# A graph kernel's first two sage passes: TensorE takes the next layer's rows directly behind the turn of the gathered rows

## The reference

```python
def _sage_conv(h, src, dst, Ws, Wn, b):
    msg = h[src]
    summed = jax.ops.segment_sum(msg, dst, num_segments=n)
    deg = jax.ops.segment_sum(jnp.ones(src.shape), dst, num_segments=n)
    neigh = summed / jnp.maximum(deg, 1.0)[:, None]
    return h @ Ws.T + neigh @ Wn.T + b
h = jax.nn.relu(_sage_conv(x, src, dst, Ws0, Wn0, b0))
prev = h
h = _sage_conv(h, src, dst, Ws1, Wn1, b1)
h = jax.nn.relu(h + prev)
return _sage_conv(h, src, dst, Ws2, Wn2, b2)
```

## Time and profile before

| what | value |
|---|---|
| median of 3 runs | 5097.33 us (5092.68 to 5098.29) |
| the profiled execution, its own time | 5105.29 us |
| its span in the profile | 5103.5 us |
| PE busy | 3761.0 us (74%) |
| DVE busy | 3758.0 us (74%) |
| ACT busy | 3214.3 us (63%) |
| POOL busy | 2811.2 us (55%) |
| granted TensorE clock, mean | 0.862 |

### The profile page before, as it was taken

One profiled execution on the slowest core, in us unless ns is written; L12 is line 12 of the kernel. 1 busy time (PEld: TensorE's weight loads), 2 busy tenths in 40 slices (PEclk: granted clock), 3 DMA queues, 4 the chain that ended last, 5 costly groups with the idle time before them and its releaser, 6 DMA issues. The chain is left out here.

```text
span 5103.5 us, 104447 instructions
## 1 busy us (share of the span) xinstructions
PE 3761.0 (74%) x23663; PEld 3105.7 (61%) x23663; DVE 3758.0 (74%) x10843; ACT 3214.3 (63%) x11475; POOL 2811.2 (55%) x2759
## 2 busy tenths in 40 slices
PE   6365889966877677768776878788687887967775
PEld 5254778855557555645674655466576776856664
DVE  1576789978869786978796868699576775746666
ACT  2022779966868686968674533278586785646554
POOL 0474767702750473067104767676564765757776
PEclk9699999988998898989776767699899998978777
DMA  8899999955975696579664446567697996762221
GB/s 177 111 290 282 363 370 312 279 146 158 287 255 148 194 285 212 161 229 291 187 183 137 152 149 206 168 215 240 211 304 254 302 305 214 246 153 59 65 66 55
DMA packets 918273, 1074.23 MB, mean 210 GB/s; under 512 B 202779, under 2 KB 565065, under 8 KB 917106
## 3 DMA queue, kind: packets, MB, share of 16 engines
q1 hardware_dynamic: 763570, 890.24, 53.5%
q0 software_dynamic: 90944, 180.06, 14.4%
q10 hardware_dynamic: 63556, 1.81, 1.8%
HBM read 509.54 MB, written 566.14 MB: 211 GB/s over the span
## 5 line engine op out<-in xcount | busy, mean ns | idle before, releaser
L2366 POOL DMA_INDIRECT H<-gat_rows,src_i x784 | 802.4, 1023 | 870.0 <-POOLq L80 631.9
L1917 POOL DMA_INDIRECT s_G<-sage_rows,src_i x588 | 603.1, 1026 | 353.7 <-issue 162.5
L1696 POOL DMA_INDIRECT r_G<-rel_rows,idx x392 | 404.8, 1033 | 166.5 <-issue 117.4
L2555 PE MATMUL p_M<-Wg,p_hT 128*128 128x132 f32 x2352 | 340.3, 289 | 61.1 <-DVE p_res L2612 47.2
L2555 PEld LDWEIGHTS p_M<-Wg,p_hT 128*128 128x128 f32 x2352 | 294.8, 194 | 108.1 <-issue 91.7
L2612 DVE SCALAR_TENSOR_TENSOR p_res<-p_M,p_rr,cg 128x132 f32<-128x132 f32 x1176 | 333.8, 346 | 2.8 <-PE p_M L2555 1.9
L1709 PE MATMUL r_t<-r_oh,relv 8*128 8x512 f32 x294 | 205.3, 784 | 171.2 <-DMA r_G<-rel_rows,idx 72.8
L1305 PE MATMUL d_S<-ones,d_sqT 128*128 128x1 f32 x1568 | 226.1, 265 | 138.6 <-DVE d_ve L1450 138.5
L2694 PEld LDWEIGHTS p_pl_p<-Wn,p_pl_h 128*128 128x128 f32 x1568 | 202.3, 195 | 206.5 <-ACT p_pl_h L2788 159.6
L2694 PE MATMUL p_pl_p<-Wn,p_pl_h 128*128 128x128 f32 x1568 | 221.2, 286 | 137.4 <-ACT p_pl_h L2788 137.3
L1305 PEld LDWEIGHTS d_S<-ones,d_sqT 128*128 128x128 f32 x1568 | 219.5, 216 | 165.9 <-issue 128.3
(11 more groups left out here) (483 smaller groups left out, 12421.8 us busy)
## 6 DMA issues: line engine op xcount, KB each, us to landing
gat_rows<-p_res SPq DMA_DIRECT2D x294, 264.0 KB
sage_rows<-p_pl_s SPq DMA_DIRECT2D x294, 256.0 KB
gat_rows<-x_row SPq DMA_DIRECT2D x98, 536.0 KB
gat_rows<-d_res SPq DMA_DIRECT2D x147, 264.0 KB
d_hs<-gat_rows SPq DMA_DIRECT2D x147, 256.0 KB
s_hT<-sage_slots_t SPq DMA_DIRECT2D x147, 256.0 KB
slot_rows<-H SPq DMA_DIRECT2D x49, 544.0 KB
x_x<-in_x SPq DMA_DIRECT2D x98, 256.0 KB
```

The lines of the kernel that those rows point to most:

```text
L1696: pool.indirect_dma_start(self.G[:, g % 4, k, :], None, table, bass.IndirectOffsetOnAxis(index[:, c:c + 1], 0), bounds_check=bound, oob_is ...
L1917: pool.indirect_dma_start(self.G[:, g % 4, k, :], None, kn.st[self.l], bass.IndirectOffsetOnAxis(kn.idx[:, c:c + 1], 0), bounds_check=boun ...
L2366: pool.indirect_dma_start(kn.H[:, c, 0:width], None, table, bass.IndirectOffsetOnAxis(index[:, c:c + 1], 0), bounds_check=bound, oob_is_er ...
L2555: mm = pe.matmul(self.pM[self.bank(b, j)][:, k // 2, (k % 2) * TW:(k % 2 + 1) * TW], self.hT[l][:, b.s2, k * P:(k + 1) * P], kn.Wg[:, l, : ...
```

## The change

One number in `SageSlots.tensor`: the place of `rows` in the turn of PE, for the two passes that are not the last.

```diff
         if self.last:
             return [(sum_squares, 5), (own, 2), (turn_back, 5), (turn, 1), (rows, 5)]
-        return [(turn, 1, kn.KG, 1), (rows, 4, kn.KG, 4), (own, 2, kn.KG, 3)]
+        return [(turn, 1, kn.KG, 1), (rows, 4, kn.KG, 1), (own, 2, kn.KG, 3)]
```

## The result

The changed kernel takes 5028.19 us (median of 4 runs, 5021.91 to 5035.27), the kernel before 5097.81 us (median of 4, 5092.68 to 5102.47). The ratio is 0.9862, with a 95% interval of 0.9849 to 0.9876: faster by 1.4%, 70 us. The forecast was 60 us less, 5037 us.

The account below looks back on a forecast made before the run. A circle of waits through PE and DVE was taken to set 6.04 us per turn; 82 x (6.04 - 5.35) = 56.6 us plus 3.6 for tails gives 60, so 5097.33 - 60 = 5037 us, range 5024 to 5070.

Parts of the forecast that it names:

- The circle and the gap: PE and DVE in s0 and s1: `rows` leaves the waiting circle, 0.89 us, and fills PE's idle 0.70 us.
- `rows` doesn't wait in its new place: PE's `rows` behind the turned rows: ACT's results come 1.8 us ahead, so the cost is 0.
- Rival B: No change, 5097 us: `rows` would wait for ACT and hold up PE's transposes, 0.8 us a turn; chance 0.06.
- PE and DVE alone: Turn in s0 and s1 allowed by these two engines: 5.17 + 0.06 = 5.23 us.
- the back edge of the loop: Every fourth turn: DVE starts `own` 0.49 us behind PE, not 0.20, costing 0.06 us on the mean.
- that fits by 0.06 us: PE's own step: `add_own` ends at S + 2.21, with 0.14 us for the semaphore, before own at S + 2.41.
- POOL: Issuing four gathers a turn in s0 and s1 takes 5.26 us, so PE can't get far below this.
- The DMA engines: Transfers of 1.84 MB per turn in s0 and s1: taken as 5.35 us, between 5.26 and 5.46.
- Tails and heads: Turns outside the 41 of each pass: three tail turns each give 6 x 0.6 = 3.6 us, heads nothing.
- What it would show: Signs in s0 and s1: turns of 5.3 to 5.4 us, `base` wait small, PE waiting for gathers, 340 to 350 GB/s.
- Rival C: Slower, up to 5163 us: ACT waits for the store of `features` from its two buffers; chance 0.05.

Follow-up runs that it names:

- Experiment 1: The changed kernel with `rows` last in PE's turn, behind `products`, instead of behind the turned rows; 5027.91 us, ratio 0.9883 to the kernel before.
- experiment 3: The changed kernel with `rows` moved in pass s0 only, s1 keeping the old order; 5044.44 us, ratio 0.9917 to the kernel before.
- Experiment 4: The kernel before, with two of the four matmuls of the turned gathered rows made twice in s0 and s1; 5081.24 us, ratio 0.9995.
- experiment 6: The changed kernel with two of the four matmuls of the turned gathered rows made twice in s0 and s1; 5007.13 us, ratio 0.9873 to the kernel before.
- experiment 8: The changed kernel with `add_own` placed first in DVE's turn; 5001.21 us, ratio 0.9863 to the kernel before.
- experiment 2: The changed kernel with `rows` third in PE's turn, between the transposes of z and own; 5059.55 us, ratio 0.9949 to the kernel before.
- Experiment 9: The kernel of experiment 8, storing only a quarter of the plain nodes' output; 5006.65 us, ratio 0.9859 to the kernel before.
- experiment 10: The kernel of experiment 8 with a quarter of the gathers left out in s0 and s1; 4977.32 us, ratio 0.9797 to the kernel before.
- Experiment 7: The changed kernel with SyncE's two stores of the plain nodes ahead of its load of z; 4998.82 us, ratio 0.9854 to the kernel before.

## Why the prediction was right

**The circle and the gap: shown.** I said that `rows` lies for 0.89 us in the circle through DVE's `own` and `base`, and would nearly fit into PE's idle 0.70 us. The turn went from 5.97 to 5.08 us, 0.89 us. Experiment 1 shows that the other side of the turned rows does nearly as well, experiment 3 that each pass gains by itself. Experiment 4 shows the gap from the other side: work put there before costs nothing.

**`rows` doesn't wait in its new place: nearly.** It waits for ACT three times in a stretch of 200 us of s1, 1.4 us in all, and not at all in that of s0. Rival B didn't come.

**PE and DVE alone: 5.23 forecast, 5.15 measured.** In s1, where PE waits least, turns are 5.08, 5.08, 5.07 and 5.36 us by turns, 5.15 on the mean. I had added 0.04 us for address instructions that cost nothing, and had the back edge of the loop at about the right size (0.06 us on the mean, 0.07 measured). I had PE's own work as the longer of the two, 5.13 against 5.08 for DVE's circle; it is the other way round, with PE's work at 4.87 us (experiments 6 and 8). This is one error seen from two sides. I took the 0.60 us from transposes to own as work; experiments 2, 6 and 8 show 0.43 to 0.46, and the rest was own waiting for `add_own`. The step "that fits by 0.06 us" was wrong: in the changed kernel own starts 0.15 us after `add_own` ends, so it is just this that the circle now runs over. It did no harm to the number, since the wait was in the 0.60 us.

**POOL: 5.26 forecast, 5.25 measured.** The first gathers of block 0 and of block 48, in s0 and in s1:

```profile
3607.88 0.99 POOL L1917 DMA_INDIRECT s_G<-sage_rows,src_i  x1 [51.45 <-POOLq L80]
...
3859.99 1.00 POOL L1917 DMA_INDIRECT s_G<-sage_rows,src_i  x1 [0.30 <-PE s_t L1928]
3892.50 0.99 POOL L1917 DMA_INDIRECT s_G<-sage_rows,src_i  x1 [27.32 <-POOLq L80]
...
4144.39 0.99 POOL L1917 DMA_INDIRECT s_G<-sage_rows,src_i  x1 [0.30 <-issue]
```

48 blocks take 252.11 and 251.89 us, 5.25 each. PE turns the last block's rows 9.4 and 9.7 us after POOL began it. That s1's 41 turns are shorter than 5.25 is no gain over POOL: s1's head was longer, 49.0 us from the first gather to block 7's turned rows against 46.7 in s0, and PE caught up.

**The DMA engines: the term that was mis-sized.** I took 5.35 us per turn instead of POOL's 5.26, halfway to 5.46, which I had from the DMA share and a ceiling of 1.05. Measured were 5.24 and 5.19, at 351 to 353 GB/s. The share went to 1.01 only, so a share of 0.95 at 305 GB/s had not meant that 95% of the capacity was taken; with 15% more traffic it rose by 6%. Experiment 9 shows that a tenth of the bytes is worth nothing. This term is the 10 us between 60 and 70: 82 turns by 0.14 us are 11 us. I had also set the 386 GB/s of the earlier pass aside for its larger pieces, which its traffic doesn't bear out (packets, MB, rate, as in the earlier trace rows):

```profile
DMA packets 12323, 21.22 MB, mean 386 GB/s; under 512 B 1405, under 2 KB 6169, under 8 KB 12314
```

These are 1.7 KB a packet and half of them under 2 KB, where the stretch of the earlier trace rows has 1.9 KB a packet and 16% under 2 KB. What the transfers alone would allow here no run shows; experiment 10 shows that 5.05 us is possible, with 64 KB less. The HBM figure of the Trainium skill (DMA: Bandwidth & Descriptors, Specifications), about 358 GB/s, would give an estimate of 5.14 us as the shortest turn (I had written 5.13). The turns of 5.24 and 5.19 us lie just above it and don't decide, but the 386 GB/s over 55 us of the earlier trace rows lies above it, so it is no ceiling for this kernel.

**Tails and heads: right in sum.** I gave 3.6 us for the tails. From block 48's turned rows to the next pass's first gather it was 25.0 us before and is 23.1 now in s0, 26.4 and 24.5 in s1: 3.8 us. The heads, for which I counted nothing, gave 2.4 us back in s0 and took 3.2 in s1.

**What it would show: a turn below 5.3.** I had written 5.3 to 5.4 us for a turn, and it was 5.24 and 5.19. The other signs came: the wait for `base` gone, POOL waiting for PE no more, PE waiting for gathers now and then, 351 to 353 GB/s, s2 and tp as long as before.

**Rival C came in a mild form and cost nothing.** ACT waits for the store of `features` 39 times, 21.1 us in all from the start of s0 on, at most 2.4 us, where before it never did. Experiment 7 takes the wait away and gains nothing, for ACT is not in the circle.

## What to carry to other kernels

On an engine that works in a fixed order, put a step that nobody in the circle waits for beside the other engine's part of the circle, not between two links of it. Read the circle from one turn of the timeline of two engines, start to start, and ask of each interval whether it is work or a wait: an interval from one start to the next can hold a wait that the list of waits doesn't name. Then price the next floor in the same unit, here 5.25 us per turn of an engine, POOL, that looked 65% busy and is at its floor at 77%, since the gain ends there. PE's busy share tells as little: it reads 98 to 99% in the changed kernel, while a turn of 5.08 us holds 4.87 us of PE's work.

## What I had not expected of the hardware

The DMA share isn't a measure of what room is left. In this kernel it was 0.95 at 305 GB/s, 1.01 at 351, and 0.98 at 316 with a tenth of the bytes left out (experiment 9), and 1.05 at 386 in the earlier pass. And the issue of a gather holds its 1.0 us, with 0.30 us between two, at 305 GB/s and at 351: POOL's mean per gather in the changed kernel is 1.31 us, as in the earlier trace rows.
